# Selective scan of a hybrid network: state rows on partitions against channels on partitions

## What is computed

```python
delta = softplus(dts + dt_bias)                 # per channel and pixel
def step(h, inp):
    d_t, x_t, B_t, C_t = inp
    dA = exp(d_t[..., None] * As)               # channel x state
    h = dA * h + (d_t * x_t)[..., None] * B_t[:, :, None, :]
    y = einsum('bkdn,bkn->bkd', h, C_t)         # sum over the 16 states
    return h, y
```

## Time and profile before

| | us |
|---|---|
| median of three runs | 963.06 |
| the three runs | 963.06, 965.89, 962.89 |
| the profiled execution's own time | 966.98 |
| its span, first to last instruction | 965.2 |

### The profile page before, as it was taken

How to read it: one execution, slowest core, us unless ns; L and a number is a source line. 1 busy time by engine, 2 the same in 40 slices (tenths; PEclk the granted TensorE clock), 3 DMA queues, 4 the chain that set the end, 5 groups by cost and what they waited for, 6 DMA issues and landing times.

```text
span 965.2 us, 8057 instructions
## 1 busy us (share of the span) xinstructions
PE 705.2 (73%) x2720; PEld 374.2 (39%) x2720; DVE 689.1 (71%) x652; ACT 357.3 (37%) x408; POOL 398.1 (41%) x204
## 2 busy tenths in 40 slices
PE   4937767676677576677777675665746759999998
PEld 3513232232232232222322221223532548888886
DVE  5369979889889889898898696694579143343432
ACT  3746336244263353452632233441410223232321
POOL 3237857768668577577685470000004100000000
PEclk9958569577695786775855877887959658999999
DMA  6030300300302103003012000502062000000000
GB/s 182 1 87 1 85 2 1 87 0 0 87 0 49 38 0 87 0 0 87 1 30 57 1 0 1 239 0 94 1 249 100 0 1 1 1 0 0 0 0 22
DMA packets 13926, 38.39 MB, mean 40 GB/s; under 512 B 2372, under 2 KB 3494, under 8 KB 13166
## 3 DMA queue, kind: packets, MB, share of 16 engines
q1 hardware_dynamic: 13904, 38.12, 13.9%
HBM read 20.73 MB, written 0.61 MB: 22 GB/s over the span
## 4 chain that ended last, share of the span: by engine, by line
PE 38%; DVE 35%; issue 13%; DMA 5%; ACT 4%; SPq 2%; POOL 1%; DVEq 1%; ACTq 0%
DVE area L1020 15%; PE ps L1588 13%; PE ps L1309 5%; DVE area L1008 5%; DMA stack<-area 4%; PE ps L1326 3%; PE ps L1601 3%; DVE area L323 2%; SPq L496 2%; PE ps L1292 2%; PE ps L1340 1%; DVE small L395 1%; PE ps L1267 1%; DVE area L990 1%; DVE area L1001 1%
## 5 line engine op out<-in xcount | busy, mean ns | idle before, releaser
L564 POOL TENSOR_TENSOR area<-area 128x1024 f32<-128x1024 f32 x126 | 324.4, 2577 | 156.5 <-DVE area L1020 156.5
L1309 PE MATMUL ps<-stack,sel 128*128 128x512 f32 x512 | 250.9, 595 | 138.2 <-DVE area L1020 83.9
L1020 DVE TENSOR_TENSOR_SCAN area<-ps,area 128x1024 f32<-128x1024 f32 x128 | 291.5, 2278 | 0.0
L695 ACT ACTIVATE ps<-ps,par_now 128x1024 f32<-128x1024 f32 x128 | 139.1, 1087 | 295.5 <-PE ps L1309 295.5
L1309 PEld LDWEIGHTS ps<-stack,sel 128*128 128x128 f32 x512 | 109.4, 254 | 316.6 <-DVE area L1020 142.1
L1008 DVE TENSOR_TENSOR area<-ps,area 128x1024 f32<-128x1024 f32 x128 | 154.7, 1208 | 57.4 <-PE ps L1309 54.2
L1588 PE MATMUL ps<-stack 128*128 128x512 f32 (+3 forms) x768 | 127.8, 326 | 0.4 <-DVE stack L1233 0.4
L1588 PEld LDWEIGHTS ps<-stack 128*128 128x128 f32 x768 | 117.0, 192 | 11.9 <-issue 2.6
L1326 PE MATMUL ps<-area,cst 128*32 128x512 f32 x512 | 96.1, 847 | 5.9 <-DVE area L1061 5.9
L422 DVE COPY area<-ps 64x1024 f32<-64x1024 f32 x32 | 39.3, 1227 | 85.6 <-PE ps L1588 85.6
L420 ACT ACTIVATE area<-ps 64x1024 f32<-64x1024 f32 x32 | 32.6, 1017 | 107.4 <-PE ps L1588 107.4
(11 more groups left out here) (282 smaller groups left out, 692.6 us busy)
## 6 DMA issues: line engine op xcount, KB each, us to landing
stack<-area SPq DMA_DIRECT2D x48, 256.0 KB, 4.6
area<-phi_scaled SPq DMA_DIRECT2D x1, 4104.0 KB, 25.3
stack<-tok SPq DMA_DIRECT2D x16, 256.0 KB, 5.0
area<-in_m_phi_dram SPq DMA_DIRECT2D x4, 1024.0 KB, 8.1
area<-phi_scaled SPq DMA_DIRECT2D x1, 4096.0 KB, 13.5
area<-in_q_t_dram SPq DMA_DIRECT2D x1, 1024.0 KB, 13.6
area<-in_dft_dram SPq DMA_DIRECT2D x1, 784.0 KB
area<-in_m_u_dram SPq DMA_DIRECT2D x1, 768.0 KB, 6.4
```

The lines of the kernel that those rows point to most:

```text
L564: pool.tensor_tensor(state[:, i % 8, :], state[:, i % 8, :], c_rep[:, b, :], MUL).then_inc(sig("weighed"), 1)
L695: act.activation(steps_pair(i), steps_pair(i), ACT.Exp, scale=par_now[:, i:i + 1]).then_inc(sig("decayed"), 1)
L1020: dve.tensor_tensor_scan(state[:, i % 8, :], steps_pair(i), drive[:, i % 4, :], 0.0, MUL, ADD).then_inc(sig("scanned"), 1)
L1309: mm = pe.matmul(ps[:, bank + h, :], sel[:, 4 * (j % 2) + v, :], stack[:, b, what, j // 2, h * HALF:(h + 1) * HALF], start=True, stop=True)
```

## The change

The unit becomes one state index for all 128 channels, so that `delta` and `delta * x` need no spreading and B and C do. There are still 16 units in a block and 128 in all. The blocks now go image by image (four directions of image 0, then of image 1), and the loops are written out, with no hardware loop.

- TensorE spreads B of a unit into banks 0, 1 or 2, 3 and C into banks 4, 5: two matmuls each, one per half of the pixels. The high and low parts of B and C (`bc_rows`) take 32 partitions for each half; the four (B or C, half) lie in four different groups of 32 partitions.
- VectorE multiplies B by `u_in` in place in PSUM (`drive_unit`), and the scan takes the decay from SBUF and the drive from PSUM. The order is drive, drive, scan, scan for a pair of units.
- ScalarE makes the decay from `delta` in SBUF (`make_decay`) and copies C out of PSUM (`copy_c`); GpSimd weighs the state with that copy (`weigh`).
- TensorE sums: `sum_state` multiplies every state by the 128 x 128 matrix `center` (layer norm's mean removal) and accumulates in banks 6, 7 over all directions and states of an image, with the state read in image order; `D * x` is the first term.
- `finish_soft`, `restack`, `stack`'s DMAs, `scan_orders`, the copies of B and C for 1,024 pixels, the rounding of `delta` and `delta * x`, and `center_first` are gone. GpSimd does the adds of softplus and `delta * x` (`soft_sum`); the first block's are VectorE's.
- Banks 4, 5 are shared by C, the projections and other jobs in a fixed order (`turns`, `shared_free`); PE does a job in the second or third pair of each block.
- Layer 1's transforms, and layer norm, gate and projection of image 0, move into the scan; the norm's scale and shift are folded into the weights of the projection (`w_out_w`, `w_out_b`), and the scale by the deviation is applied behind it.

```diff
+        JOBS = {}                      # Z_AT, ROWS_AT = 1, 2
+        for _n in range(1, BLOCKS):
+            JOBS[8 * (_n - 1) + Z_AT] = ("z", _n)
+            JOBS[8 * (_n - 1) + ROWS_AT] = ("rows", _n)
+        JOBS[8 + 4], JOBS[8 + 6], JOBS[2 * 8 + 4], JOBS[4 * 8 + 4] = ("spec", 0), ("spec", 1), ("skip", 0), ("var", 0)
+        turns = [("z", 0), ("c", 0), ("c", 1)]
+        for _m in range(PAIRS):
+            if _m in JOBS:
+                turns.append(JOBS[_m])
+            turns += [("c", _u) for _u in (2 * _m + 2, 2 * _m + 3) if _u < UNITS]
...
+        FREED = {"z": "relu_ready", "c": "c_copied", "rows": "rows_ready", "gate": "z_ready", "spec": "spec_out",
+                 "skip": "skip_added", "var": "var_logged"}
...
 GpSimd
+            def weigh(u):
+                pool.wait_ge(sig("scanned"), u + 1)
+                pool.wait_ge(sig("c_copied"), u + 1)
+                at = state[:, u % STATES, :]
+                pool.tensor_tensor(at, at, c_sb[:, u % COPIES, :], MUL).then_inc(sig("weighed"), 1)
...
+            for m in range(PAIRS):
+                n, p = divmod(m, 8)
+                weigh(2 * m)
+                if p in (2, 3, 4, 5) and n < BLOCKS - 1:
+                    soft_sum(n + 1, p - 2)
+                if 2 * m + 1 < UNITS - 1:
+                    weigh(2 * m + 1)
...
 ScalarE
+            def rows_round(n):
+                act.wait_ge(sig("rows_done"), n + 1)
...
+                act.activation(high(rows_high), ps[:, (4 if n else 2), :], ACT.Copy).then_inc(sig("rows_rounded"), 1)
+            def make_decay(u):
...
+                wait(act, sig("scanned"), u - DECAYS + 1)
+                act.activation(decay[:, u % DECAYS, :], delta[:, n % 2, :], ACT.Exp, bias=floors[:, k, i:i + 1],
+                               scale=par_sb[:, k, i:i + 1]).then_inc(sig("decayed"), 1)
+            def copy_c(u):
+                act.wait_ge(sig("c_spread"), u + 1)
+                wait(act, sig("weighed"), u - COPIES + 1)
+                act.activation(c_sb[:, u % COPIES, :], banks(4), ACT.Copy).then_inc(sig("c_copied"), 1)
...
+            for m in range(PAIRS):
...
+                    make_decay(2 * m + 4)
+                if p == Z_AT and n < BLOCKS - 1:
+                    soft(n + 1, "z")        # Abs and Relu
+                elif p == ROWS_AT and n < BLOCKS - 1:
+                    rows_round(n + 1)
...
+                    copy_c(2 * m + 2)
...
+                    make_decay(2 * m + 5)
...
+                    copy_c(2 * m + 3)
...
 VectorE
+            def split_rows(n):
+                dve.wait_ge(sig("rows_rounded"), n + 1)
...
+                dve.scalar_tensor_tensor(bc_rows[:, n % 2, :], rows_high, con("low"), ps[:, (4 if n else 2), :],
+                                         MUL, ADD).then_inc(sig("rows_ready"), 1)
+            def drive_unit(u):
...
+                dve.wait_ge(sig("b_spread"), u + 1)
+                dve.tensor_tensor(drive_pair(u), drive_pair(u), u_in[:, n % 2, :], MUL).then_inc(sig("driven"), 1)
+            def scan_unit(u):
...
+                wait(dve, sig("summed"), u - STATES + 1)
+                dve.tensor_tensor_scan(state[:, u % STATES, :], decay[:, u % DECAYS, :], drive_pair(u), 0.0,
+                                       MUL, ADD).then_inc(sig("scanned"), 1)
...
+            for m in range(PAIRS):
+                n, p = divmod(m, 8)
+                drive_unit(2 * m)
+                drive_unit(2 * m + 1)
+                scan_unit(2 * m)
+                scan_unit(2 * m + 1)
+                if p == ROWS_AT and n < BLOCKS - 1:
+                    split_rows(n + 1)
...
 TensorE
+            def spread(u, what, bank):
+                n, b, k, i = block_of(u)
+                for h in range(2):
+                    at = 32 * (2 * what + h)
+                    mm = pe.matmul(ps[:, bank + h, :], sel[at:at + 32, i, :], bc_rows[at:at + 32, n % 2, :],
+                                   start=True, stop=True)
+            def spread_b(u):
...
+                wait(pe, sig("scanned"), u - 1)
+                spread(u, 0, (0, 2)[u % 2]).then_inc(sig("b_spread"), 1)
+            def spread_c(u):
...
+                shared_free("c", u)
+                spread(u, 1, 4).then_inc(sig("c_spread"), 1)
+            def sum_state(u):
...
+                    pe.wait_ge(sig("weighed"), u + 1)
+                for h in range(2):
...
+                    mm = pe.matmul(ps[:, 6 + h, :], con("center"), part(image_order(state[:, u % STATES, :], k), k, h),
+                                   start=False, stop=(u % (UNITS // 2) == UNITS // 2 - 1), skip_group_check=True)
...
+            EARLY = {0: ((), ()), 1: ((), (0,)), 2: ((1,), (2, 3)), 3: ((4,), (5, 6))}
+            def sums_of(m):
...
+                return ((), (2 * m - 1, 2 * m)) if m in JOBS else ((2 * m - 1,), (2 * m,))
...
+            for m in range(PAIRS):
+                before, beside = sums_of(m)
+                pe.wait_ge(sig("scanned"), 2 * m + 1)
+                if 2 * m + 2 < UNITS:
+                    spread_b(2 * m + 2)
+                if m in JOBS:
+                    job(*JOBS[m])
...
+                for u in before:
+                    sum_state(u)
+                pe.wait_ge(sig("scanned"), 2 * m + 2)
+                if 2 * m + 3 < UNITS:
+                    spread_b(2 * m + 3)
+                if 2 * m + 2 < UNITS:
+                    spread_c(2 * m + 2)
+                for u in beside[:1]:
+                    sum_state(u)
+                if 2 * m + 3 < UNITS:
+                    spread_c(2 * m + 3)
+                for u in beside[1:]:
+                    sum_state(u)
+                if m == 0:
+                    gate(0)
+                    gate(1)
+            sum_state(UNITS - 1)
```

More of the change, by code:

```diff
@@ L44 @@
 CONST = {}
-for _name, _n in (("ident", P), ("pair", P), ("red", 4 * 32), ("mean", P), ("center", P),
+for _name, _n in (("ident", P), ("pair", P), ("pick", NS), ("low", 1), ("mean", P), ("center", P),
                   ("heads", P), ("split", P), ("merge", 4 * P), ("rank", E), ("sign", 1)):
@@ L557, in slot @@
-            def slot(k, s):
-                n, b, i = split_slot(k, s)
-                if ends(k, b) and i >= GROUPS - 2:
-                    return
-                if i == 0:
-                    wait(pool, sig("c_ready"), n + 1)
-                wait(pool, sig("scanned"), GROUPS * n + i + 1)
-                pool.tensor_tensor(state[:, i % 8, :], state[:, i % 8, :], c_rep[:, b, :],
-                                   MUL).then_inc(sig("weighed"), 1)
-                if i == 7 and not ends(k, b):
-                    rest(n + 1)
-                if i == 10 and not ends(k, b):
-                    low(n + 1)
@@ L1273, in gate @@
             def gate(b):
+                if b == 0:
+                    shared_free("gate", 0)
+                else:
+                    pe.wait_ge(sig("xc_ready"), 2)
                 for h in range(2):
-                    for part in range(2):
-                        mm = pe.matmul(ps[:, 6 + h, :], front_hl[:, part, 10 * DI:11 * DI],
-                                       pads[b][:, 16 * h + 1:16 * h + 17, 1:1 + W], start=(part == 0), stop=(part == 1))
-                mm.then_inc(sig("z_done"), 1)
@@ new lines, in gate, with project_z, project_rows @@
+                mm.then_inc(sig("gate_done"), 1)
+            def project_z(n):
+                b, k = divmod(n, ND)
+                shared_free("z", n)
+                pe.wait_ge(sig("xc_ready"), b + 1)
+                for h in range(2):
+                    mm = pe.matmul(ps[:, 4 + h, :], w_z[:, k, :], part(scan_order(xc[:, b, :], k), k, h),
+                                   start=True, stop=True)
+                mm.then_inc(sig("z_done"), 1)
+            def project_rows(n):
+                b, k = divmod(n, ND)
+                if n:
+                    shared_free("rows", n)
+                for what in range(2):
+                    for h in range(2):
+                        at = 32 * (2 * what + h)
+                        mm = pe.matmul(ps[at:at + 32, (4 if n else 2), :], w_rows[:, k, what, :],
+                                       part(scan_order(xc[:, b, :], k), k, h), start=True, stop=True)
+                mm.then_inc(sig("rows_done"), 1)
@@ new lines, in job @@
+            def job(kind, i):
+                if kind == "z":
+                    project_z(i)
+                    return
+                if kind == "rows":
+                    project_rows(i)
+                    return
+                shared_free(kind, i)
+                if kind == "spec":
+                    pe.wait_ge(sig("ab_in"), 16)
+                    pe.wait_ge(sig("dft_in"), 16)
+                    for r in range(2):
+                        for h in range(2):
+                            mm = pe.matmul(ps[64 * h:64 * h + 64, 4 + r, :], ab_sb[:, i, :],
+                                           half(dft_sb[0:2 * KK, r, :], h), start=True, stop=True)
```

(18 more changed lines are left out.)

783 lines of the change are left out of this document (343 added, 440 removed).

## The result

| | before | after |
|---|---|---|
| median, us (runs) | 964.01 (4) | 987.08 (4) |
| lowest and highest | 962.89 and 965.89 | 985.25 and 989.47 |
| the profiled execution's own time and span | 966.98, 965.2 | 989.47, 987.6 |

The ratio is 1.0239, 95% interval 1.0207 to 1.0271: 2.4% slower, where 894 us was forecast and 945 was the end of the range.

A forecast was written before the change was run, and what follows sets the result against it. VectorE was taken to bound the scan. First drive 41.1, loop 424 + 6 + 5 + 16 + 3 + 7 + 4 + 25 = 490, then 11: norm at 542 instead of 611.2, 69 less, so 963.1 - 69 = 894 us; range 848 to 945.

The forecast's parts named there:

- the price of the sum: PE's `sum_state` in the loop: four records, 1.72 us, or 3.44 at the low clock; two sums per pair.
- the prediction's own inequality: At the odd drive: 0.1 us, spread and 1.72 us sum must fit a 2.19 us scan; 0.1 to spare with overlap.
- Rival 2: `sum_state` between B's two spreads: PE becomes the bound, 54% of pairs at the low clock, 976 us; chance 0.15.
- Cold pairs: Loop pairs with PE at the low clock, PE-bound: one per block, 8 x 3.1 = 25 us.
- Job pairs: Pairs with next-block jobs: PE late, `split_rows` waits, 16 us; `split_rows` itself 5; second image's start 4.
- odd-drive pinch: Odd drive waits for its spread behind `sum_state`: between 0 and 17 us over 64 pairs, 6 taken.
- other jobs: Four other jobs at the start of each block's preparation delay a drive by about 0.7 us: 3 us.
- GpSimd 7: In four pairs with an added instruction GpSimd has 7.1 us of work against 6.62: 1 us per block, 7 in all.
- The start: Ahead of the scan: SiLU ends at 28.2, first drive starts at 41.1 us, 19.6 earlier than 60.7.
- Behind the scan: From last scan to layer 1's norm: 9.6 us at high clock, 12 at low, 11 taken; before 27.7.
- rival 3: VectorE's drive in place in PSUM is slow, 1.07 us more at the scan's rate: 1000 us; chance 0.05.
- rival 4: GpSimd is the bound in the loop, if reading `x` turned is slow there: about 930 us; chance 0.03.

The follow-up runs named there:

- Run 3: A separate program without the network, operands read at various steps: a float32 matmul record took 0.43 us at step 1, 0.86 at step 32.
- Run 1: Kernel after the change, with `sum_state` reading the two turned directions straight (turning back left out): 920.33 us, ratio 0.9529.
- run 8: Projections read x straight, against the changed kernel with GpSimd writing image order, a sum ahead of C's spread and `split_rows` behind the next drives: 903.09 us, ratio 0.9337.
- run 5: In the `z` pair PE sums once before C's spread, against the changed kernel with GpSimd writing image order: 915.40 us, ratio 0.9467.

## Why the prediction was wrong, and where it was right

**The step that failed** is the price of the sum in the first paragraph on PE: "`sum_state` is four records: 1.72 us, or 3.44 at the low clock", the same for every direction, so that what a record takes hangs on the clock alone. It rests on "L1340's eight took 5.70 us: 0.86 us a record at 1.2 GHz, 0.43 at 2.4, which makes about five of the one and three of the other". The clock was guessed from the durations there and not read, and how the operand is read was left out. L1340 runs twice in that stretch, and the trace has the clock of both. The stretches of PE alone in the kernel before:

```profile
537.80:539.50 1.70, 1.67 (x2) 0.50 0.03 10
...
537.80:541.80 4.00, 3.97 (x5) 0.50 0.01 4
...
542.00:543.50 1.50, 1.50 (x5) 1.00 0.00 0
544.30:549.00 4.70, 4.70 (x8) 1.00 0.00 0
```

The second set of eight took 5.32 us from 544.29 on, all of it at clock 1.00. At 0.43 us a record it would have taken 3.4. Its first two matmuls read direction 2 in turned order through `in_image_order`, its last two a straight operand: four records of 0.86 and four of 0.43 make 5.2. The first set begins with direction 0, turned as well, at the low clock: two records in 1.67 us, so a turned record takes about 0.86 us at either level. That set is the one that the prediction read, and by luck its count even holds: the clock was 0.50 up to 541.8 us and 1.00 from 542.0 on, which leaves four turned records and one straight one at the low level and three straight ones at the high. It could not tell the two causes apart; the second set could. The trace was there, the lines of the code that build the operand were there, and the change puts just this kind of operand on the busiest path of the loop. Run 3 is the price with nothing around it.

So `sum_state` costs 1.72 us in half of the blocks and 3.44 in the other half, at the full clock. In the prediction's own inequality (0.1 + spread + sum inside one scan of 2.19 us) the turned sum, 1.72 us longer with 0.1 to spare, comes some 1.6 us late in every pair; the pairs show 1.53 (8.15 less 6.62). PE's own work adds up to the same: in the time line around 125 us it is 0.47 and 0.43 us from the start of a group of spreads to the sum behind it, and 3.62 from there to the next spreads, 8.14 for the two of a pair. So in the turned blocks PE is the bound. Rival 2 named the place, the sum between the two spreads of B, and "PE becomes the bound", and gave it 976; it had the wrong cause, and with it the wrong count; that its 976 lies near the 987 measured is luck. It was to decide from 30 pairs of 64 at the low clock. After the change 21 of the 63 measured pairs had a mean clock below 0.9; the 35 plain pairs (first, and fourth to eighth of a block) that did not were still 55 us over their 6.62.

The rest, term by term. Run 1 has the sums as the prediction meant them, so its pairs size the other terms; the excess over 6.62 us is added up over its 63 pairs, split by position in the block and by mean clock below or above 0.9.

- *Cold pairs*: 25 forecast, as 8 of 3.1 us, each 9.7 us long. Measured 15 plain ones with 20 us together, most of them 7.5 to 8.2 us long and a single one 9.6. The term's size was right, its two factors were not. One cold and the following warm pair of run 1:

```profile
359.17:367.32 8.15, 6.89 (x17) 0.79 0.00 0
367.32:373.94 6.62, 5.36 (x17) 1.00 0.01 2
```

- *Job pairs*: 16 + 5 for `z`, `rows` and `split_rows`, and 4 for the second image's start. Measured 12 us in the second and third pairs of the first block and 42 in those of the others: 54 for 25, the other mis-sized term. Part of it is the half rate of the projections (run 8: 10 us, of which 2.4 lie ahead of the scan). PE's 2 us of idling and what follows from it in the next pair are another 10 by run 5, which took them away. A third part is argued only: the decay, taken at 1.0 us, is 1.23, and ScalarE's rounding stands behind one. The mechanism, "PE enters the next pair 2 us late" and VectorE waits at `split_rows`, is in the time line above as it was written; the wait there is 3.75 us and not 2.
- *Everything else in plain warm pairs* (odd-drive pinch 6, other jobs 3, GpSimd 7): 7 us of 16 forecast. The halves of a spread do overlap: the four records of two spreads (B and C, both halves, four groups of 32 rows) take 0.50 us, the two of one 0.49.

```profile
338.66 0.50 PE L1320 MATMUL ps<-stack,sel 32*128 32x512 f32 x4
...
341.00 0.49 PE L1320 MATMUL ps<-stack,sel 32*128 32x512 f32 x2
```

- *The start*: 44.7 for 41.1. SiLU ends at 29.3 and not at 28.2 (1.1), the projection of `z` is turned (3.65 for 1.98: 1.7), `u` reads `x` turned (1.99 for 1.22: 0.8). Together 3.6, all of the miss.
- *Behind the scan*: 10.8 for 11. *VectorE's own work*: drive 1.22, scan 2.27, pair 6.62, as forecast; rival 3 did not come. *GpSimd*: 2.36; rival 4 did not come: the product that reads `x`, turned in three of seven blocks, took 2.34 to 2.36 us in all of them. *DMAs*: next to none left in the loop (a share of 0.00 or 0.01 in the stretches shown).

The account closes. Loop of the kernel after: 64 pairs at 6.62, and 153 us over them. Run 1: 82 over them. The difference, 71 us, is the turned sums alone, which the sum of the prediction had at nothing; the other 82 stand for the prediction's 66. With the front, 894 + 71 + 16 + 4 = 985, against 987 measured.

## What to carry to other kernels

Price an operand by how it is read, not only by its size: a float32 matmul whose moving operand is read with a step of 3 or more runs at two thirds to half of its full-clock rate (0.68 to 0.92 us for 0.43), and an engine with time to spare that writes the turned order (here GpSimd, at no extra cost) takes that off the matmul's path. When a group of equal instructions has two durations, read the granted clock of each stretch and the access pattern of each instruction before calling it the clock. And a wait taken out of one queue is worth something only if the engine that it waited with is not late anyway: `split_rows` alone gave nothing.

## What the runs showed of the hardware

- TensorE's moving operand, 512 columns of float32 at clock 1.00, per record: step 1 and -1 0.43 us, 2 0.45, 3 0.68, 4 0.90, 8 0.92, 16 0.86, 32 0.86, 33 0.91. One-pass: 0.23, and 0.43 to 0.48 from step 2 on.
- 1,024 columns turned: ScalarE 1.94 us reading or writing so, 1.06 straight. VectorE with two inputs 1.90 with one operand turned, 1.23 straight. GpSimd 2.36 when it writes turned, the same as straight (2.34), but 2.85 with the first input turned and 3.60 with both. The second input turned alone costs nothing either: `soft_sum` of the kernel after (L573) reads `x` so in three of its seven blocks, and all seven took 2.34 to 2.36. The rows of run 3 (L172 both inputs, L170 the first, L171 the output, L169 none) and that one:

```profile
L172 POOL TENSOR_TENSOR yb<-x,f 128x1024 f32<-128x1024 f32 x4 | 14.4, 3598 | 0.3
L170 POOL TENSOR_TENSOR yb<-x,f 128x1024 f32<-128x1024 f32 x4 | 11.4, 2845 | 0.3
...
L171 POOL TENSOR_TENSOR yb<-x,f 128x1024 f32<-128x1024 f32 x4 | 9.5, 2364 | 0.3
L169 POOL TENSOR_TENSOR yb<-x,f 128x1024 f32<-128x1024 f32 x4 | 9.3, 2338 | 377.2 <-DVEq L162 376.9
...
L573 POOL TENSOR_TENSOR area<-area 128x1024 f32<-128x1024 f32 x7 | 16.4, 2348 | 0.0
```

- ScalarE's Exp with scale and bias per partition took 1.23 us for 1,024 columns from SBUF, its copy out of PSUM 1.02.
- A drive written back in place into PSUM costs VectorE next to nothing: 1.22 us against 1.21 into SBUF.
